# Joining four seams between stages of a Macaron transformer kernel, and dealing PSUM banks by a rough clock

## The reference

```python
x = x + 0.5 * L0_ffn(layernorm(x))     # silu(x Wg * gs) * (x Wu * us), then Wd * ds; weights rounded to FP8, width 1536
x = x + L0_attn(layernorm(x))          # 16 query heads, 4 key/value heads of 32, biases, rope, causal
x = x + 0.5 * L0_ffn(layernorm(x))     # the same weights again
x = x + 0.5 * L1_ffn(layernorm(x))     # silu(x Wg) * (x Wu), then Wd; width 2048
x = x + L1_attn(layernorm(x))          # 16 heads of 32, causal, no bias
x = x + 0.5 * L1_ffn(layernorm(x))
```

## Time and profile before

| | us |
|---|---|
| median of 3 runs | 2704.14 (2702.6 to 2717.95) |
| the profiled execution's own time | 2707.04 |
| its span, first to last instruction | 2705.3 |
| TensorE busy with matmuls | 2620.1 (97%) |
| VectorE, ScalarE, GpSimd busy | 1368.5, 1078.1, 637.4 |
| mean granted TensorE clock | 0.993 of full |

### The profile page before, as it was taken

How to read it: one execution, slowest core, us unless ns; L and a number is a source line. 1 busy time by engine, 2 the same in 40 slices (tenths; PEclk the granted TensorE clock), 3 DMA queues, 4 the chain that set the end, 5 groups by cost and what they waited for, 6 DMA issues and landing times.

```text
span 2705.3 us, 36133 instructions
## 1 busy us (share of the span) xinstructions
PE 2620.1 (97%) x13216; PEld 1999.4 (74%) x13216; DVE 1368.5 (51%) x2784; ACT 1078.1 (40%) x1989; POOL 637.4 (24%) x1102
## 2 busy tenths in 40 slices
PE   6999899999999999999999999999999999999999
PEld 4788766666657888888888888666766588888887
DVE  7787566756655445533333344566356543333333
ACT  7555355655563223311211133556455632111111
POOL 3333432332222234411111121222122321111110
PEclk9999999999999999999999999999999999999999
DMA  4222121122111110000000002322132100000001
GB/s 144 71 71 74 39 65 33 36 56 48 36 37 52 35 43 9 31 24 24 24 26 29 24 9 64 86 60 61 37 81 62 43 32 24 26 29 24 24 16 63
DMA packets 59679, 119.80 MB, mean 44 GB/s; under 512 B 11632, under 2 KB 12656, under 8 KB 59504
## 3 DMA queue, kind: packets, MB, share of 16 engines
q1 hardware_dynamic: 59504, 117.51, 15.1%
HBM read 62.42 MB, written 13.63 MB: 28 GB/s over the span
## 4 chain that ended last, share of the span: by engine, by line
PE 82%; DVE 3%; issue 2%; ACT 2%; DMA 2%; POOL 2%; SPq 1%; DVEq 0%; ACTq 0%; POOLq 0%
PE psum L741 62%; PE psum L862 9%; PE psum L826 5%; PE psum L844 4%; PE psum L750 1%; DVE s1a0masked L1203 1%; PE psum L872 1%; DMA raw<-in_o 1%; DVE s4a1masked L1203 1%; POOL x L1312 0%; PE psum L882 0%; SPq L1399 0%; DVE tmp L1173 0%; ACT s4a1e L1032 0%; POOL rstd L1290 0%
## 5 line engine op out<-in xcount | busy, mean ns | idle before, releaser
L741 PE MATMUL psum<-hA_hi,wmem 128*128 128x256 f32 (+1 forms) x1536 | 404.0, 335 | 1.1 <-DVE s1a0negmax L1203 0.8
L741 PE MATMUL psum<-hA_lo,wmem 128*128 128x512 f32 (+1 forms) x864 | 294.2, 341 | 0.0
L741 PEld LDWEIGHTS psum<-hA_hi,wmem 128*128 128x128 f32 x1536 | 269.5, 191 | 32.9 <-DVE s1a0negmax L1203 1.8
L1032 ACT ACTIVATE s1a0e<-psum,p_scale 128x384 f32<-128x384 f32 (+5 forms) x384 | 203.5, 579 | 103.6 <-PE psum L844 102.5
L1032 ACT ACTIVATE s4a1e<-psum,p_scale 128x384 f32<-128x384 f32 (+5 forms) x384 | 204.7, 580 | 99.8 <-PE psum L844 97.7
L1203 DVE CUSTOM_DVE_ANT_0 s4a1masked<-psum,mask_q 128x512 bf16<-128x512 f32 (+7 forms) x256 | 189.9, 751 | 93.8 <-PE psum L826 91.0
L1203 DVE CUSTOM_DVE_ANT_0 s1a0masked<-psum,mask_q 128x512 bf16<-128x512 f32 (+7 forms) x256 | 189.5, 752 | 64.6 <-PE psum L826 62.3
L1155 DVE SCALAR_TENSOR_TENSOR x<-psum,x 128x512 f32<-128x512 f32 x256 | 175.5, 688 | 86.1 <-PE psum L741 81.9
L1126 DVE TENSOR_TENSOR s5f1prod<-psum,s5f1silu 128x512 f32<-128x512 f32 x64 | 44.3, 692 | 299.0 <-PE psum L741 299.0
L1126 DVE TENSOR_TENSOR s3f1prod<-psum,s3f1silu 128x512 f32<-128x512 f32 x64 | 44.3, 692 | 294.5 <-PE psum L741 294.5
L741 PE MATMUL psum<-s3f1w,s3f1a 128*128 128x512 f32 x768 | 181.1, 391 | 0.9 <-POOL s3f1w L1302 0.9
(11 more groups left out here) (196 smaller groups left out, 5066.5 us busy)
## 6 DMA issues: line engine op xcount, KB each, us to landing
s1a0qst<-s1a0qs SPq DMA_DIRECT2D x96, 128.0 KB, 2.4
s4a1qst<-s4a1qs SPq DMA_DIRECT2D x96, 128.0 KB, 2.4
s4a1kst<-s4a1ks SPq DMA_DIRECT2D x96, 128.0 KB, 2.4
raw<-in_gate SPq DMA_DIRECT2D x44, 256.0 KB, 2.7
raw<-in_up SPq DMA_DIRECT2D x44, 256.0 KB, 2.7
raw<-in_down SPq DMA_DIRECT2D x44, 256.0 KB, 2.7
rounded<-s0f0w SPq DMA_DIRECT2D x24, 256.0 KB, 2.0
s2f0w<-rounded SPq DMA_DIRECT2D x24, 256.0 KB, 5.0
```

The costliest lines, as they stand in the source:

```text
L741: ins = pe.matmul(out_, w, m, start=n == 0, stop=n == len(terms) - 1)
L1032: act.activation(T[s]["e32"][:, begin_ + z * pw:begin_ + (z + 1) * pw - skip], src, ACT.Exp, bias=p_scale[:]).then_inc(sem["exp"], 1)
```

## The change

In the last group before attention, the down steps of the last two chunks are held back and handed to `attention`, which deals six of them between its first pieces and two (LATE_DOWNS) between its first rows. At the end of attention the next stage's "begin" and first gate and up products are dealt between the last steps, at the ticks EARLY_AT; that next stage goes on with two normalization starts at each tick in its second chunk. "begin" waits for what `gave_way` lists (last products of the stage before, not its last writes of x), and a new step "open" waits for x later. SBUF tiles are allocated in another order, with a gap in f1, so that what is still in use lies elsewhere. `Pace` keeps a finishing time for each engine from fixed durations, and `bank_turns` takes the banks whose emptying ends first by that clock. The parts left out hold the other kinds of steps in Pace, the order in which tiles are allocated, and the same "begin" and "open" for the other engines.

```diff
@@ -50,7 +50,10 @@
 AHEAD = 13
 FIRST_ROW, LAST_ROW = -AHEAD % ST, (ST - 1 - AHEAD) % ST
 PV_LAG = 7
+EARLY_AT = (0, 1, 4, 7, 8)
+LATE_DOWNS = 2
 E32 = 5632
+GAP = 8192
 STACK = 3 * HD
...
@@ -134,16 +141,27 @@
             return ffn_weights(s, 0, ("gate", "up"))
         return group_weights(s, 0) + group_weights(s, 1)
 
+    def first_products(s):
+
+        mts = MTS[STAGES[s]]
+        steps = [[("begin", s)]]
+        for m in range(mts):
+            steps.append([("gu", s, 0, 0, m)] + [("a_lo", s, 0, 0, m - 1)] * (m > 0))
+        return steps + [[("a_lo", s, 0, 0, mts - 1)]]
+
     def ffn(s):
+
         kind = STAGES[s]
         groups, mts = GROUPS[kind], MTS[kind]
-        plan.append(("begin", s))
+        after_heads = s > 0 and not is_ffn(s - 1)
+        if not after_heads:
+            plan.append(("begin", s))
         if s:
             weights.waiting += ffn_weights(s, 0, ("down",))
-        pending = None
+        pending, catching_up = None, False
 
         def tick(point):
-            norms.tick(NORMS_AT[kind][point])
+            norms.tick(2 if catching_up else NORMS_AT[kind][point])
             weights.tick(WEIGHTS_AT[kind][point])
 
         def down(g, c):
@@ -155,8 +173,9 @@
 
         for g in range(groups):
             for c in range(NC):
-                if g == 0 and c < 2:
-                    norm(s, c + 2)
+                if g == 0 and c == 0:
+                    norm(s, 2)
+                    norm(s, 3)
                 if g == 0:
                     norms.finish(last_norm[s, c])
...
@@ -169,24 +188,42 @@
                         weights.waiting += first_weights(s + 1)
                     if c > 1:
                         norm(s + 1, c - 2)
+                catching_up = after_heads and (g, c) == (0, 1)
                 for m in range(mts):
-                    plan.append(("gu", s, g, c, m))
-                    if m > 0:
-                        plan.append(("a_lo", s, g, c, m - 1))
-                    if m + 1 < mts:
+                    if not (after_heads and (g, c) == (0, 0)):
+                        plan.append(("gu", s, g, c, m))
+                        if m > 0:
+                            plan.append(("a_lo", s, g, c, m - 1))
+                    if m + 1 < mts and not (after_heads and (g, c) == (0, 0)):
                         tick(m)
+                if after_heads and (g, c) == (0, 0):
+                    weights.tick(2)
+                    pending = (g, c)
+                    continue
                 plan.append(("a_lo", s, g, c, mts - 1))
                 tick(mts - 1)
-                if pending:
+                if pending and not (into_heads(s) and (g, c) == (groups - 1, NC - 1)):
                     down(*pending)
-                pending = (g, c)
-        down(*pending)
+                    pending = None
+                if not pending:
+                    pending = (g, c)
+        left = []
+        if into_heads(s):
+            weights.finish(last_weight[s, groups - 1, "down"])
+            left = [[[("down", s, groups - 1, c, i)]] for c in (NC - 2, NC - 1) for i in range(CT)]
+        else:
+            down(*pending)
         weights.flush()
-
-    def attention(s):
+        return left
+
+    def attention(s, left):
         grouped = STAGES[s] == "a0"
-        norms.flush()
         plan.append(("begin", s))
+        downs = Beside(plan)
+        downs.waiting += left
+        while norms.busy(last_norm[s, 0]):
+            norms.tick()
+            downs.tick()
         plan.append(("v_ones", s))
         plan.append(("k_ones", s))
         v_weights = Beside(plan)
@@ -212,8 +249,15 @@
...
@@ -212,8 +249,15 @@
         first = Beside(plan)
         first.waiting += group_jobs(0)
         while first.waiting or first.running:
-            first.tick()
+            norms.tick()
+            if norms.busy(last_norm[s, 1]) and any(("piece", s, 0, "q", 2) in job[0]
+                                                   for job in first.waiting[:1]):
+                first.tick(0)
+            else:
+                first.tick()
             v_weights.tick()
+            if len(downs.waiting) > LATE_DOWNS:
+                downs.tick()
         v_weights.flush()
         for j in range(HPG):
             for n in "qk":
@@ -226,7 +270,11 @@
                       - (u + wait - 1) * tiles // (AHEAD + wait))
             if u >= 0:
                 row_unit(u)
+            if u % 2 == 0:
+                downs.tick()
         side.flush()
+        downs.flush()
+        plan.append(("open", s))
 
         beside = defaultdict(list)
 
@@ -288,9 +336,17 @@
                     if at == when:
                         for m in names_of_group(s, g + 1):
                             plan.append(("stack", s, g + 1, m, j))
+        early = first_products(s + 1)
         for unit in behind:
             times_v(*unit)
-        side.flush()
+        ticks = 0
+        while side.waiting or side.running:
+            side.tick()
+            if early and ticks in EARLY_AT:
+                plan.extend(early.pop(0))
+            ticks += 1
+        for steps in early:
+            plan.extend(steps)
 
     plan += [("x_in", t) for t in range(CT)]
     norm(0, 0)
...
@@ -373,25 +434,147 @@
                         "y_turn", "y_tp", "oproj"))
 
 
+class Pace:
+
+
+    def __init__(self):
+        self.free, self.done = defaultdict(float), defaultdict(float)
+
+    def work(self, engine, length, *needs):
+        begin = max([self.free[engine]] + [self.done[n] for n in needs])
+        self.free[engine] = end = begin + length
+        return end
+
+    def run(self, step, banks):
+
+        kind, s, *where = step
+        work, done = self.work, self.done
+        grouped = STAGES[s][0] == "a" and STAGES[s] == "a0"
+        f0 = STAGES[s] == "f0"
+        if kind == "ln_stats":
+            done[step] = work("pool", 1.1)
+            done["stats", s, where[0]] = done[step] = max(done[step], work("dve", 0.87) + 1.1)
+        elif kind == "ln_norm":
+            done["norm", s, where[0]] = work("act", 0.81, ("stats", s, where[0]))
+        elif kind == "ln_tp":
+            done[step] = work("pe", 0.5, ("norm", s, where[0]), *banks)
...
+            done[step] = work("dve", 0.69, ("ln_hi", s, where[0]))
+        elif kind == "gu":
+            n = 8 if f0 else 12
+            gate = done[step] = work("pe", n * 0.23, *banks)
+            done[step] = work("act", 0.68, step)
+            silu = done[step]
+            done["up", step] = work("pe", n * 0.23)
+            done[step] = work("dve", 0.72, step, ("up", step))
+            done["a_hi", step] = work("act", 0.63, step)
+        elif kind == "a_lo":
+            done[step] = work("dve", 0.69, ("a_hi", ("gu",) + step[1:]))
+            done["a", s, where[0], where[1]] = done[step]
...
+        elif kind == "key":
+            width = SEQ - where[1] * P
+            cols = max(width, 2 * P)
+            cols = cols if cols <= CH else cols // 2
+            done[step] = work("pe", cols / 2250 + 0.02, ("m_in", s, where[0]), *banks)
+            done[step] = work("act", cols / 1230 + 0.26, step)
+        elif kind == "pv":
+            width = SEQ - where[1] * P
+            done[step] = work("pe", width / 2250 + 0.1,
+                              ("key", s, *where, 0 if width <= CH else 1), *banks)
+        elif kind == "take":
+            done[step] = work("act", 0.6, ("pv", s, where[0], ST - 1))
+        elif kind == "y_turn":
+            done[step] = work("pe", 0.5, ("take", s, where[0]), *banks)
+        elif kind == "y_fin":
+            done[step] = work("dve", 0.6, ("y_turn", s, where[0]))
+        elif kind == "y_tp":
+            done[step] = work("pe", 0.5, ("y_fin", s, (where[0] + 1) * HPG - 1), *banks)
+            done[step] = work("act", 0.6, step)
+            done["yT", s, where[0]] = done[step] = work("dve", 0.69, step)
+        elif kind == "oproj":
...
+    holder = {}
+    pace = Pace()
+    release = {}
+    for step in plan:
         width = banks_wanted(step)
-        if not width:
-            continue
-        first = min(range(BANKS - width + 1), key=lambda i: max(empty[i:i + width]))
-        mine = list(range(first, first + width))
-        banks[step] = mine
-        earlier[step] = [(used[bank], banks[used[bank]].index(bank)) for bank in mine
-                         if bank in used]
-        if step[0] == "pv":
-            then = at[("take",) + step[1:-1]]
-        else:
-            then = at[(EMPTIED_BY.get(step[0], step[0]),) + step[1:]]
-        for bank in mine:
-            used[bank], empty[bank] = step, then
+        needs = []
+        if width:
+            now = pace.free["pe"]
+
+            def cost(i):
+                waits = max(empty[i:i + width])
+                return waits
+
+            first = min(range(BANKS - width + 1), key=cost)
+            mine = list(range(first, first + width))
+            banks[step] = mine
```

(81 more changed lines are left out.)

105 lines of the change are left out of this document (80 added, 25 removed).

## The result

The changed kernel takes 2695.86 us (median of 9 runs, 2689.55 to 2700.43) against 2704.14. I had forecast 28. The profiled execution took 2691.6 us, 15.4 less than the 2707.0 of before, so even the two profiles differ by little more than half of the forecast.

The account below looks back on a forecast made before the run. TensorE, busy 2620.1 of 2705.3 us, was taken as the bound, leaving its idle time and half-clock loss. Terms 8 + 8 + 0.8 + 2 + 9 = 28 us off the median 2704.1 gave 2676; range 2668 to 2684, 8-in-10 range 2662 to 2694.

Parts of the forecast that it names:

- Banks: Attention stages: dealing banks by the rough clock wins 9 us, 60% of 14.2; ends -10 and 17.
- the row pairs wait for VectorE itself: Rival for the attention stages: the bank clock brings nothing, giving 2685 us; chance 0.16.
- Clock: Seams: half of the half-clock busy time is lost, 4.2 us at A, 3.4 at B, 2.9 at D.
- The prediction's bound for A: Seam A, s0 to s1: idle time and lost clock together can give at most about 17.4 us.
- Seam A: From s0 to s1: earlier begin and tables, with downs filling the wait, win 8 us; ends 3 and 14.
- the row's time: Seam A: the first row of s1 comes at 331.5 us, 6.5 us earlier.
- the blocked subtractions: Seam A: VectorE's subtractions beside POOL's adds cost 6 x 0.45 = 2.7 us.
- Seam C: From s3 to s4: downs dealt between pieces cover a 0.77 us wait, winning 0.8 us; ends -1 and 0.8.
- Seam B: From s1 to s2: early gate and up steps cover the waits and earlier scales, winning 8 us; ends 4 and 8.3.
- Seam D: From s4 to s5: only two gate and up steps, winning 2 us; ends -1 and 5.7.
- The wait before oproj: Seam D: with nothing between y_tp and oproj, a wait of 2.2 us where 2.8 were.
- the worst case of a whole add: Seam A: a whole POOL add before each of eight subtractions would cost 10 us in place of 2.7.

Follow-up runs that it names:

- three timed pairs: Kernels with and without the new bank dealing: kernel before, 2699.41 against 2704.14 us; changed kernel, 2695.86 against 2696.91; early begin only, 2686.28 against 2691.12.
- experiment 8: Experiment 4's kernel with every step's bank written out from that kernel's own trace: 2680.50 us, 0.9916 of the kernel before.
- experiment 12: Experiment 5's kernel with two late downs at Seam A (2677.49 us), its banks written out from its own trace: 2684.65 us.
- Experiment 4: Changed kernel with the last down steps left in place ahead of attention, begin still early: 2684.23 us, 0.9922 of the kernel before.
- experiment 9: Changed kernel with two of the held-back downs put ahead of the first normalization behind begin: 2687.73 us, 0.9940 of the kernel before.
- experiment 10: Changed kernel with downs held back at Seam A alone, in place at Seam C: 2689.09 us, 0.9949 of the kernel before.
- experiment 6: Changed kernel with downs in place and no early products at either seam, begin early, banks by the rough clock: 2686.28 us, 0.9936 of the kernel before.
- experiment 5: Experiment 4's kernel with early products and doubled normalizations at Seam B alone, not at Seam D: 2680.29 us, 0.9915 of the kernel before.
- experiment 7: Experiment 6's kernel with the old dealing of banks by order of steps, leaving the early begin: 2691.12 us, 0.9958 of the kernel before.

## Why the prediction was wrong

The waits at each seam were mostly read rightly from the profile, but two steps failed. The dealing of banks was priced at time that its waits did not give back, and holding the down steps back, which I had put at nothing beside its gain, cost 11 us (6 to 16), the largest single error. Besides, lost clock was counted twice as high as the runs have it. By the steps of the sum:

- **Banks** (9 us): the two profiles show 3.3, and the three timed pairs 5.1, 2.4 and 5.9. I took 60% of the 14.2 us in which a better bank had been free as time that could be had. In the traces of those pairs the new dealing did take away 10 to 12 us of such waits (16.5 to 6.0, 19.3 to 7.5, 15.6 to 5.5 by the count above), but all waits at banks fell only by 0.2, 3.8 and 0.7 us. Experiments 8 and 12 show that even banks written out from a trace leave 22 to 27 us of waits. This goes most of the way to the rival "the row pairs wait for VectorE itself": with one bank's wait gone, the next row meets an engine that is as late as before. The rival's "nothing" is too low all the same.
- **Clock**: I counted lost half-clock time as if every run had it: 3.4 us at B, 2 at A, about 1.7 at D. The profile of before had 0.993, the other runs 0.9946 in the mean, the changed kernel's runs 0.9959. A us at half clock is half a us of time lost, so the difference of 0.0013 over 2700 us is 3.5 us of time, or 7 us more at half clock, where I had counted 7 us of time. (The prediction's bound for A also left out the spell at 352, 1.7 us.) From one profile to the other the stretches fell from 37.5 to 17 us, which is 10 us of time. So 7 of the profiles' 15.4 us belong to these two executions, and their own times say the same: that of before stands 2.9 us over its median, that of after 4.2 under its own.
- **Seam A** (8 us): the row's time was forecast to 0.2 us, partly by luck, and the seam gave 6.9 in the profile. The failed part is one that I costed at nothing: the held-back downs take the ticks and the matmuls away between which the next stage's normalizations had run. TensorE meets the transposes first and waits 2.31 and 1.45 us at A. And the downs then lie before VectorE's pieces, with the blocked subtractions that I had priced. Experiment 4 shows that the seam wins more without them; how its cost divides between the transposes and VectorE's queue stays open.
- **Seam C** (0.8 us): the same wait, 2.21 us, and a loss. "TensorE was busy anyway" overlooked what the order of the other engines does. Experiments 9 and 10 remove the wait, and C takes 101.3 and 101.4 us.
- **Seam B** (8 us): 8.3 in the profile. Right in size, but for another reason: three quarters are the early begin's, which the forecast had only as a condition of the products; by themselves these bring 2.3 there, and 3.9 between the profiles of experiments 6 and 5.
- **Seam D** (2 us): a loss of 1.4 in the profile, and experiment 5 is 2 us better without it. The wait before oproj was as forecast. I had written that the down weights' wait would stay. It grew, and the doubled normalizations were late: with two product steps gone from between, the same loads have 11 us less time by the plan.

The prediction took from the Trainium skill (SBUF — State Buffer, Terms) that VectorE and GpSimd share an exclusive port. The trace agrees: five of eight subtractions beside POOL's adds took 0.37 to 0.42 us more, the size of the row that I had, and none the worst case of a whole add.

One way through the experiments leads from the kernel before to the changed one (7, 6, 5, 4, changed): early begin 11 us, dealing 6, early products at B about 6 (of which the profiles show 2.3 and 3.9), less 2 at D, less 11 for the held-back downs. Such a chain must end at the 10 us measured, so its sum proves nothing; each step of it has an uncertainty of 5 us, and the 2 at D rests on the profiles. The seams without the dealing give 7.6, so what the early begin won was nearly all given back by holding the downs. Open is why holding costs 11 us in timed runs when the profiles show 5.5 at the two seams; 2.4 us of it are the clock (0.9968 without holding, 0.9959 with), and the rest wasn't tried.

## What to carry to other kernels

Where engines stand for a load at a seam, first move the load's own condition forward: here that was most of the gain (11 us), and holding compute back to cover a wait that the earlier load had already taken away cost about as much (11 us). When side work sits between other steps, holding those steps back also brings the side work's consumers closer to its producers: look at what each tick had in between. And time that a trace shows as lost at a wait for a buffer is only the buffer's if its reader isn't the one that is late: test it by writing the best buffers out by hand before you price it.

## What the runs showed of the hardware

Runs of the changed kernel differ by 11 us, and the granted clock goes with it: 2689.55 us at 0.997 and 2700.43 at 0.994. Spells of half clock, of 3.4 us or a multiple, mostly stand at or behind waits of TensorE, but waits of the same size bring one or none. From 290 us on, the changed kernel's profile has eleven waits over 1 us. Three of them have a spell (2.02 us at 344, with 6.8 us of half clock; 1.50 at 550; 2.15 at 2181), the other eight, up to 2.47 us at 2153, have none, and the spell at 502 has no wait longer than 0.70 us in the 8 us ahead of it. A profile's own spells are thus a sample, and I should have weighed them by the clock of all runs.
